# Sums that TensorE adds up run three units behind the scans instead of two, and are copied out a unit later

## What is computed

```python
x = silu(causal_depthwise_conv(x, conv_w, conv_b))
x_dbl = x @ x_proj_w.T
dt = softplus(x_dbl[..., :DT_RANK] @ dt_proj_w.T + dt_proj_b)
...
def step(h, inputs):
    dA_t, dBx_t, C_t = inputs
    h = dA_t * h + dBx_t              # (512 channels, 16 states)
    y = jnp.einsum('bdn,bn->bd', h, C_t)
...
y = selective_scan(...) ; y = y * silu(z) ; return y @ out_proj_w.T
```

## Time and profile before

| | |
|---|---|
| median of 3 runs | 1387.17 us (1381.75 to 1388.46) |
| the profiled execution | 1381.12 us, span 1379.3 us |
| scans | about 45 to 905 us of the span |
| routing and experts | about 905 to 1379 us |
| mean granted TensorE clock | 0.949 |

### The profile page before, as it was taken

How to read it: one execution, slowest core, us unless ns; L and a number is a source line. 1 busy time by engine, 2 the same in 40 slices (tenths; PEclk the granted TensorE clock), 3 DMA queues, 4 the chain that set the end, 5 groups by cost and what they waited for, 6 DMA issues and landing times. The chain is left out here.

```text
span 1379.3 us, 20920 instructions
## 1 busy us (share of the span) xinstructions
PE 1224.6 (89%) x7128; PEld 931.6 (68%) x7128; DVE 900.5 (65%) x1065; ACT 768.4 (56%) x1461; POOL 918.0 (67%) x511
## 2 busy tenths in 40 slices
PE   8978888989797878798787889899999999999996
PEld 4445555656555555565566644458999999999996
DVE  3898999998898989999999999962111111111110
ACT  4678877778787697877887675613111111111111
POOL 1899999999988989999999889822222222222211
PEclk9999999999998989989899899999999999999998
DMA  5666666556555465655566554608998898888882
GB/s 199 209 192 181 174 178 188 170 190 198 154 162 193 153 185 167 207 178 169 175 205 181 187 174 151 192 17 323 356 319 323 318 314 309 318 320 314 323 305 45
DMA packets 110124, 297.03 MB, mean 215 GB/s; under 512 B 10033, under 2 KB 22066, under 8 KB 94530
## 3 DMA queue, kind: packets, MB, share of 16 engines
q1 hardware_dynamic: 100370, 277.59, 58.5%
q0 software_dynamic: 9648, 18.09, 6.5%
HBM read 277.82 MB, written 9.96 MB: 209 GB/s over the span
## 5 line engine op out<-in xcount | busy, mean ns | idle before, releaser
L1397 POOL TENSOR_TENSOR arena<-arena 128x1024 f32<-128x1024 f32 x192 | 456.6, 2397 | 50.3 <-DVE arena L1117 36.3
L484 PE MATMUL ps_y<-ident,arena 128*128 128x128 f32 x1792 | 254.2, 289 | 62.2 <-POOL arena L1397 61.1
L484 PEld LDWEIGHTS ps_y<-ident,arena 128*128 128x128 f32 x1792 | 217.0, 149 | 129.9 <-POOL arena L1397 88.8
L1449 POOL DMA_INDIRECT out_x<-arena x39 | 61.8, 1585 | 305.1 <-ACT arena L1045 238.5
L893 ACT ACTIVATE ps_de<-arena,An 128x512 f32<-128x512 f32 x196 | 134.7, 688 | 150.7 <-DVE arena L1104 144.6
L893 ACT ACTIVATE arena<-arena,An 128x512 f32<-128x512 f32 x316 | 218.5, 710 | 0.1
L1331 DVE TENSOR_TENSOR arena<-ps_du,arena 128x512 f32<-128x512 f32 x39 | 27.0, 692 | 227.9 <-PE ps_du L742 227.9
L1381 POOL TENSOR_TENSOR arena<-arena 128x1024 f32<-128x1024 f32 x67 | 160.8, 2399 | 6.1 <-DMA arena<-bc_scratch 5.5
L742 PE MATMUL ps_y<-arena 128*128 128x128 f32 x1248 | 153.3, 276 | 0.5 <-ACT arena L1033 0.5
L1089 DVE TENSOR_TENSOR ps_u<-ps_du,arena 128x512 f32<-128x512 f32 x196 | 136.8, 698 | 22.1 <-DVE arena L1129 10.1
L742 PEld LDWEIGHTS ps_y<-arena 128*128 128x128 f32 x1248 | 149.3, 193 | 2.9 <-ACT arena L1033 0.7
(11 more groups left out here) (242 smaller groups left out, 2010.7 us busy)
## 6 DMA issues: line engine op xcount, KB each, us to landing
arena<-bc_scratch SPq DMA_DIRECT2D x256, 512.0 KB, 4.6
arena<-in_W SPq DMA_DIRECT2D x117, 1024.0 KB, 8.1
arena<-arena POOLq DMA_DIRECT2D x15, 512.0 KB, 4.9
arena<-in_cd SPq DMA_DIRECT2D x16, 256.0 KB, 5.4
out_x<-arena SPq DMA_DIRECT2D x17, 128.0 KB, 5.0
arena<-in_xT SPq DMA_DIRECT2D x2, 1024.0 KB, 6.2
arena<-in_w2c SPq DMA_DIRECT2D x1, 2048.0 KB, 9.1
diag<-in_dd SPq DMA_DIRECT2D x16, 128.0 KB, 5.0
```

The costliest lines, as they stand in the source:

```text
L484: t = e.matmul(Y[j][:, part], src[:, part], ident[:, :], start=False, stop=stop, is_transpose=True, skip_group_check=True)
L1397: e.tensor_tensor(hc[:, i % NP, :, :], hh[:, i % NH, :, :], c, ALU.mult).then_inc(gp_hc, 1)
L1449: e.indirect_dma_start(out, bass.IndirectOffsetOnAxis(dest[:, i:i + 1], 0), yo[:, i % 3, :], None, compute_op=ALU.add).then_inc(l_add, 16)
```

## The change

TensorE adds unit i - 3 in iteration i instead of i - 2 (LAG = 3). Its loop would then be one iteration longer; instead, in iteration NU - 4 = 252 it adds two units (249 and 250), and from there on unit i - 2, so the end of its program stands as before. ScalarE copies a group's sums at i + 4 (EV = 4), in the iteration with n = 3, and at the end of that iteration's work instead of right behind `decay`; the first group's copy is now at the same place as the others.

```diff
-NR, NH, NP, KD, LAG, EV, NW = 3, 5, 4, 6, 2, 3, 3
+NR, NH, NP, KD, LAG, EV, NW = 3, 5, 4, 6, 3, 4, 3
+def adds_at(i):
+
+    if i == NU - 4:
+        return (i - LAG, i - LAG + 1)
+    return (i - LAG,) if i < NU - 4 else (i - LAG + 1,)
...
-            for i in range(NU + LAG):
+            for i in range(NU + LAG - 1):
...
                 if i >= LAG:
-                    add(i - LAG)
+                    for k in adds_at(i):
+                        add(k)
...
             for i in range(NU):
-                if i == EV + 15:
-                    evac_turned(15)
                 decay(i)
...
-                if i > EV + 15 and (i - EV) % 16 == 15 and i - EV < at(3, 32):
-                    evac_turned(i - EV)
-                    if not kept_turned(unit(i - EV)[0]):
-                        evac(i - EV)
                 for w in range(2):
...
                 if i - 4 in TILE_AT:
                     tile_T(*TILE_AT[i - 4])
+                if i >= EV + 15 and (i - EV) % 16 == 15 and i - EV < at(3, 32):
+                    evac_turned(i - EV)
+                    if not kept_turned(unit(i - EV)[0]):
+                        evac(i - EV)
```

## The result

| | before | changed |
|---|---|---|
| median of 20 runs | 1385.1 us (1378.83 to 1391.74) | 1390.5 us (1381.89 to 1393.6) |
| ratio to before, 95% interval | | 1.0032 [1.0016, 1.0047] |
| the profiled execution | 1381.12 us, clock 0.949 | 1391.79 us, span 1389.8 us, clock 0.942 |

Two things stand behind these numbers, and they lie in different places. The scans, where the change works, ended 1.2 us earlier in the profiled execution instead of 11. The routing behind them, where it changes nothing, took 12.6 us longer there. A second set of 12 runs did not repeat the loss: its ratio is 1.0004 [0.9983, 1.0025].

A forecast was written before the change was run, and what follows sets the result against it. VectorE and GpSimd, each 93% busy, bound the scans, with VectorE setting the pace. Terms 5 + 6.9 - 0.5 = 11.4 us off the profiled 1381.1 gave 1369.7, so a median of 1375 us (1367 to 1381; whole range 1357 to 1391).

The forecast's parts named there:

- TensorE's wait for GpSimd at the add: In the scans, TensorE's waits for GpSimd's product ahead of an add all but vanish, from 61.1 to under 15 us.
- VectorE's waits for TensorE's transposes: In the scans, VectorE's waits for turned inputs fall from 11.6 to about 7 us; 5 us won, bounds 0 and 11.6.
- the 28.2 us: VectorE's waits in the scans for ScalarE's decays and TensorE's turned inputs, the pool from which the reordering can pay.
- The copies: ScalarE's copies of a group's sums, later and behind the decay, let decays start sooner: 6.9 us won in the scans.
- the last add is long done: At ScalarE's copy, a unit later and behind the decay of n = 3, the group's last add no longer causes waiting.
- the full iteration that the prediction described: ScalarE's iteration 99: silu and two table loads, 3.83 us, then 3.3 us of copies ahead of decay 100; 0.9 us lost.
- The next wait, 0.5 us: In the scans, new GpSimd stalls for TensorE's later adds, mainly at group starts: 0.5 us lost, bounds 0 and 22 us.
- Sum for the scans: Scans end some 11 us earlier: 5 + 6.9 - 0.5 = 11.4 us won.
- The experts: Behind the scans, 905 to 1379 us: the change touches nothing, 474 us as before.
- rival 1: In the scans, nothing to gain, as GpSimd may pace where VectorE no longer waits: 1385 us (1380 to 1391), chance 0.20.
- Rival 2: In the scans, TensorE's transposes run at the low clock oftener, undoing the gain: about 1387 us, chance 0.08.
- Rival 3: In the scans, the late copy holds up TensorE and the next group's sums: slower, 1396 us, chance 0.15.

The follow-up runs named there:

- the cut kernels: Kernel before and changed kernel, each ended behind the scans and output blocks, without routing, experts and last four tiles: 914.62 and 913.73 us, five runs each.
- hoist: Whole changed kernel, with TensorE's last add of a group first in iteration n = 2, transposes back first in n = 3: 1381.3 us (0.9972), second set 1379.67 us (0.9957).

## Why the prediction was wrong

It said 1375 us (its terms give 1375.8) and faster by over 0.5% with 0.56; the median was 1390.5 us, slower than before by 0.3%, inside the range of 1357 to 1391 at its very end. That it lay inside is luck: the profiles put what the changed kernel lost behind the scans, for which the prediction had no term, and the second set doesn't repeat the loss. The failed step is the term of the copies. By its own steps:

- **TensorE's wait for GpSimd at the add** (forecast under 15 us): right, 61.1 to 3.0 us.
- **VectorE's waits for TensorE's transposes** (11.6 to about 7, 5 us won): right in mechanism, 8.1 us, so 3.5 won (2.7 between the cut kernels). The term was a little large. The pool it was taken from was read loosely: what is idle on VectorE beside the 28.2 us isn't all short spacing, since 10.1 us of it are waits for its own product ahead of the next `u`.
- **The copies, 6.9 us**: this step failed; measured 0. It rested on "the last add is long done". The change moves both the copy and the add by one unit, so their distance stayed, and in TensorE's order the add stands behind whatever TensorE waits for in that iteration: second scans (24.1 and 16.5 us above) and side work. ScalarE's waits ahead of the copies were to fall from 19.1 to under 5 us and were 20.0, and VectorE's for the decays from 16.6 to about 9 and stayed at 16.6.

  Place by place the sum was nearly right, for the places it looked at. The stalls of units 18, 83, 115, 131, 179 and 227 went, 6.3 us as summed, and unit 19's 1.83 went whole; unit 36 kept its own (0.65), and unit 100, costed at 0.9 us of loss, went from 1.98 to 2.70. What it had at nothing were the places to which the wait would go: 2.75 us at unit 132, 1.1 more at 86, 1.0 at 236, 0.9 at 116, 0.5 more at 134, and 1.4 at a first scan. The largest, in ScalarE's timeline ahead of the decay of unit 132 and in VectorE's, with unit 100 for comparison:

```profile
480.47 1.09 ACT L932 ACTIVATE arena<-ps_y 128x512 f32<-128x512 f32 x2 [1.65 <-PE ps_y L491]
483.55 1.08 ACT L938 ACTIVATE arena<-ps_y 128x512 f32<-128x512 f32 x2 [1.99 <-PE ps_y L484]
```

```profile
372.90 1.28 DVE L1110 TENSOR_TENSOR_SCAN arena<-ps_de,hlast,arena 128x512 f32<-128x512 f32 x1 [2.70 <-ACT arena L901]
...
485.88 1.22 DVE L1110 TENSOR_TENSOR_SCAN arena<-ps_de,arena 128x512 f32<-128x512 f32 x1 [2.75 <-ACT arena L901]
```

  At unit 132 ScalarE stands 3.6 us for the add and for the transposes back, and a stall of 2.74 us was there again in the second execution. At unit 100 the copies waited 0.3 us; the loss there is the full iteration that the prediction described. The smaller ones were not followed to their causes. That the distance between add and copy is what counts is shown from both sides: with the copy moved alone VectorE's waits for decays were 9.8 us, and with the adds put first 11.8.
- **The next wait, 0.5 us**: wrong in place. GpSimd's wait for the add of n = 0 stayed small (1.0 + 0.5 + 0.4 us), but `last_gated`, which waits for the same semaphore, cost 2.5 us, five times what was allowed for all of them, and was not looked for.
- **Sum for the scans**: 11.4 us forecast; 1.2 us by the profiles, 0.9 by the cut kernels, neither clear of nothing. Less won at `first_u` (1.5), nothing at the copies (6.9) and 2.0 more of new waits make 10.4 of the missing 10.2 to 10.5. That it closes so well is luck: it takes one execution of each kernel at its word and leaves out 2.0 us of new waits for GpSimd's `u`, 1.2 more at L1168 and 1.7 that went at L1070.
- **The experts**: as forecast, 433.6 us against 434.5. The routing, in the same stretch of the forecast, took 12.6 us more.
- **The rivals.** In the scans it went by rival 1's number (nothing to gain) for another reason than it gave: GpSimd's waits for VectorE stayed at 36.0 us, so it didn't pace, and hoist shows that there was something to gain. Rival 2 was wrong where it was put: 0.93 in the scans as before. The Trainium skill, "TensorE: Matmul & The Clock Gate", section "HAM oscillation — how this bites in real kernels", from which it came, speaks of idle gaps; behind the scans the clock was low while TensorE's modelled busy time was 33.22 of 34.00 us, so no such gap is seen there. Rival 3's mechanism exists (6.2 us when the copy moves alone) but isn't what this change does.
- **Not foreseen at all**: that the routing takes 42.7 to 55.3 us from run to run. The prediction set the profiled execution 6 us below the median as a constant. With 20 runs of before the median was 1385.1 us, so the distance was 4, and it was no property of the kernel: that execution had the shortest routing of all those profiled, 42.7 us.

## What to carry to other kernels

When a producer and its consumer move by the same step, the wait between them stays: ask what stands ahead of the producer in its engine's order, and move that. List every instruction that waits on the moved semaphore, those that occur once too; one such cost 2.5 us here. And where the expected effect is below the spread of a kernel's runs, cut the kernel behind the stage in question. Five runs of each of the two cut kernels lay within 3.4 and 3.9 us, 20 of each whole one within 11.7 and 12.9. The cut runs rule out a gain of 11 us; a difference of 1 us needs more.

## What was not expected of the hardware

TensorE's granted clock stayed at 1.2 GHz for 34.1 us without a break while TensorE's modelled busy time was 98% of the stretch, and in other executions of either kernel for 17.1, 20.5 or 3.4 us at the same place. It fell at 919.1 us. From 905 to 919 us TensorE had been at the high clock and busy for 13.98 of the 14.00 us, at the last with the router's small matmuls, of which these are two rows of the changed kernel's timeline:

```profile
917.46 0.61 PE L706 MATMUL ps<-wg,arena 128*128 128x8 f32 x4
918.00 0.38 PE L707 MATMUL ps<-arena 1*128 1x8 f32 x2
```

The work in the stretch is mostly short matmuls and single rows. The Trainium skill, "TensorE: Matmul & The Clock Gate", section "Seeing it yourself", warns that trace events of the clock have been seen to be unreliable and should be cross-checked. Here the durations agree with them: the same 64 matmuls took 7.27 us in one execution (at the high clock) and 13.78 in the other, close to double. That the small matmuls are the cause was not tested by itself.
